# Three stages of a one-core, eight-layer kernel: gating cut into pieces, a last phase split by 128-row blocks, and a sixteenth of the softmax exponentials moved from ScalarE to VectorE

## What is computed

```python
# first attention: 16 heads, a window of 64 earlier rows, learned "bond" and "damage" logits
strain = disp_win - disp[:, :, :, None, :]
bond_act = gelu(strain @ W_strain + rel_emb @ W_pos)
damage = sigmoid((gelu(strain @ W_dmg + b_dmg) @ W_dmg_out)[..., 0] + b_dmg_out[0])
logits = (bond_act @ W_bond)[..., 0] - 10.0 * damage      # masked before row 0
out = einsum('bntd,bntde->bnte', softmax(logits), val_win) @ W_cproj

# gated layer: 8 experts, the one of the largest gate logit modulo 8
probs = softmax(x @ Wg + bg); idx = argmax(probs); p = probs[idx]
h = relu(einsum('bsd,edf->besf', x, We) + be)
out = h[expert idx % 8] * p

# last attention: 16 heads of 8, 2048 keys by 2048 queries
attn = softmax(q @ k.T * d ** -0.5) * (s / sqrt(s - 1.0))
out = (attn @ v) * s ** -0.5 ; out @ w_o.T * hid ** -0.5
```

## Time and profile before

| | us |
|---|---|
| median of 3 runs (2976.29 to 2985.98) | 2984.93 |
| the profiled execution's own time | 2982.17 |
| its span, first to last instruction | 2980.4 |

### The profile page before, as it was taken

How to read it: one execution, slowest core, us unless ns; L and a number is a source line. 1 busy time by engine, 2 the same in 40 slices (tenths; PEclk the granted TensorE clock), 3 DMA queues, 4 the chain that set the end, 5 groups by cost and what they waited for, 6 DMA issues and landing times. The chain is left out here.

```text
span 2980.4 us, 33149 instructions
## 1 busy us (share of the span) xinstructions
PE 2389.2 (80%) x12605; PEld 833.9 (28%) x12605; DVE 1860.6 (62%) x2713; ACT 2010.5 (67%) x2036; POOL 1070.7 (36%) x408
## 2 busy tenths in 40 slices
PE   3677777757666666766999889998769789999995
PEld 1122222334222222333222241222434422222223
DVE  5788898857999999864888528896350401112114
ACT  4999999813633333234899758997431379999991
POOL 5999999711099999531001300013000000000000
PEclk8899999978888888787999998999889889999997
DMA  2012111110144444102202100101010120210001
GB/s 75 1 43 62 67 43 43 43 53 8 28 176 168 163 162 152 68 4 78 41 12 37 35 7 1 18 6 45 8 40 0 35 65 18 41 27 18 15 6 28
DMA packets 64985, 144.64 MB, mean 49 GB/s; under 512 B 13091, under 2 KB 27791, under 8 KB 64112
## 3 DMA queue, kind: packets, MB, share of 16 engines
q1 hardware_dynamic: 64816, 142.40, 16.5%
HBM read 117.92 MB, written 24.25 MB: 48 GB/s over the span
## 5 line engine op out<-in xcount | busy, mean ns | idle before, releaser
L674 POOL TENSOR_TENSOR l0a_diff_pool<-l0a_A,l0a_a_of_t 128x2048 f32<-128x2048 f32 x128 | 531.7, 4191 | 34.3 <-ACT l0a_a_of_t L689 33.0
L1933 ACT ACTIVATE l2x_pT<-ps 128x1024 f32<-128x1024 f32 x512 | 495.7, 1021 | 14.5 <-PE ps L1892 12.6
L1933 ACT ACTIVATE l3he_pT<-ps 128x1024 f32<-128x1024 f32 x512 | 496.0, 1021 | 6.5 <-PE ps L1892 4.6
L1262 PE MATMUL ps<-l1s_hc,all_ident 128*128 128x512 f32 x512 | 288.7, 718 | 153.2 <-POOL l1s_hc L1233 97.6
L657 DVE SCALAR_TENSOR_TENSOR l0a_diff_dve<-l0a_A,l0a_pos,ps 128x512 f32<-128x512 f32 x512 | 344.8, 741 | 29.7 <-PE ps L532 29.7
L1224 POOL TENSOR_TENSOR l1s_dBx<-l1a_dtx,l1a_Bs 128x1024 f32<-128x1024 f32 x128 | 297.7, 2357 | 111.9 <-POOLq L958 111.9
L1248 ACT ACTIVATE ps<-l1a_dt,l1a_A 128x1024 f32<-128x1024 f32 x128 | 143.0, 1118 | 268.0 <-DVE l1s_hc L1307 215.7
L1892 PE MATMUL ps<-l2m_Qs,l2m_Ks 75*128 75x512 bf16 x1024 | 273.9, 392 | 9.8 <-PEq L2215 9.8
L1892 PE MATMUL ps<-l3h_Qs,l3h_Ks 75*128 75x512 bf16 x1024 | 269.3, 386 | 12.8 <-DVE ps L1981 12.8
L1906 PE MATMUL ps<-l2x_pT,l2m_Va 128*9 128x512 f32 x2048 | 272.5, 605 | 1.2 <-ACT l2x_pT L1933 1.2
L1906 PE MATMUL ps<-l3he_pT,l3h_Va 128*9 128x512 f32 x2048 | 269.2, 598 | 0.6 <-ACT l3he_pT L1933 0.6
(11 more groups left out here) (462 smaller groups left out, 3347.8 us busy)
## 6 DMA issues: line engine op xcount, KB each, us to landing
l1a_Bs<-l1a_bc SPq DMA_DIRECT2D x64, 512.0 KB, 3.6
l1s_Cs<-l1a_bc SPq DMA_DIRECT2D x64, 512.0 KB, 4.8
l0a_band_rows<-l0a_band SPq DMA_DIRECT2D x32, 512.0 KB, 5.2
l0a_band<-l0a_exps SPq DMA_DIRECT2D x16, 512.0 KB, 5.1
l2m_Ks<-l2m_parts SPq DMA_DIRECT2D x36, 128.0 KB
l2m_Qs<-l2m_parts SPq DMA_DIRECT2D x72, 64.0 KB
l3h_Qs<-l3h_parts SPq DMA_DIRECT2D x72, 64.0 KB
l0a_band<-l0a_zero SPq DMA_DIRECT2D x8, 512.0 KB, 4.8
```

Of the source, the lines that this page charges most:

```text
L674: pool.tensor_tensor(out, window(s), atb[:, p % 2, :].unsqueeze(1).broadcast_to([P, 4, CH]), ALU.subtract).then_inc(diff_pool, 1)
L1262: mm = pe.matmul(g.ps[:, (4 + 2 * h + q) * CH:(5 + 2 * h + q) * CH], g.ident[:, :], hc[:, m % NHC, q * CH:(q + 1) * CH], start=(n == 0), s ...
L1933: act.activation(pT[:, turn % NPT, :], g.ps[:, slot * QC:(slot + 1) * QC], ACT.Exp).then_inc(expd, 1)
```

## The change

It does three things.

1. **Last attention.** In each segment key block 7 leaves the sequence. ACT makes the exponentials of 15 blocks; the four turns of block 7 go to DVE, one after each of the blocks at places 0, 3, 6 and 9. Their scores are put behind two other turns' scores in PE's list; DVE reads them out of PSUM (`taken`), and makes the exponential as a power of two and a polynomial in ten instructions over 128x1024. The values of block 7 are multiplied right behind those at places 13 (first half of the columns) and 14 (second half). `finish` of the segment before now stands behind the four exponentials on DVE.
2. **First attention.** Only the last phase's end is rewritten, by blocks: each block's exponential as soon as its maxima are subtracted (four of 128x512), its own two DRAM writes, its own load; SP's order is write 0, write 1, load 0, write 2, load 1, write 3, load 2, load 3. Normalising, transposing, projecting and adding go by pairs of blocks. On DVE the copies of the phase before for units 0 to 3 come before the last logits, those for 4 to 7 after the maxima.
3. **Gated layer.** `gate` is cut into four pieces; one piece for the next quarter follows each block's `choose`. ACT's exps(q) moves behind mask(4q + 1), probability(q) behind choose of the second block, and `y` gets 4 places.

```diff
@@ bond_attention, PE, after the last slot: instead of tail(w, off) for two more phases
+                for i in range(4):
+                    values(LAST - 1, i)
+                for b in range(LB):
+                    logits_transpose(LAST, b)
+                for i in range(4, BU):
+                    band_transpose(LAST - 1, i)
+                for i in range(4, BU):
+                    values(LAST - 1, i)
+                for b in range(4):
+                    for i in (2 * b, 2 * b + 1):
+                        band_transpose(LAST, i)
+                    if b == 2:
+                        late_o_transpose(0)
+                    if b == 3:
+                        late_project(0)
+                    for i in (2 * b, 2 * b + 1):
+                        values(LAST, i)
+                late_o_transpose(1)
+                late_project(1)
@@ VectorE
+                for i in range(4):
+                    band_copy(LAST - 1, i)
+                logits(NT // TPG - 1)
+                for b in range(LB):
+                    subtract_max(LAST, b)
+                for i in range(4, BU):
+                    band_copy(LAST - 1, i)
+                normalise(LAST - 1)
...
+                late_add(0)
+                late_normalise(1)
+                late_o_copy(1)
+                late_add(1)
@@ ScalarE
-                exps(NPH - 1)
+                for b in range(LB):
+                    act.wait_ge(emptied, use("l", LAST, b) + 1)
+                    act.activation(E[:, b, :, :], E[:, b, :, :], ACT.Exp).then_inc(late_exp, 1)
@@ SyncE
+                def load(b):
+                    sp.wait_ge(late_written[b], 32)
+                    sp.wait_ge(filled, use("b", LAST - 1, 2 * b + 1) + 1)
+                    sp.dma_start(bn[:, b, :, :].rearrange("p u h -> p (u h)"), band[LAST % 2, b]).then_inc(loaded[b], 16)
+                write(0)
+                write(1)
+                load(0)
+                write(2)
+                load(1)
+                write(3)
+                load(2)
+                load(3)
@@ gated_experts
-        y = r.sb("y", [P, 2, C])
+        y = r.sb("y", [P, 4, C])
...
-                exps(0)
                 for q in range(NCH):
                     onehot_copy(q)
                     mask(4 * q + 1)
+                    exps(q)
                     bias_copy(q)
-                    if q + 1 < NCH:
-                        exps(q + 1)
                     mask(4 * q + 3)
...
-                gate(0)
+                gate_parts = (gate_max, gate_equal, gate_first, gate_hot)
+                for part_of_gate in gate_parts:
+                    part_of_gate(0)
                 for q in range(NCH):
-                    if q + 1 < NCH:
-                        gate(q + 1)
-                    for b in range(4 * q, 4 * q + 4):
-                        choose(b)
-                        if b == 4 * q:
+                    for b in range(4):
+                        choose(4 * q + b)
+                        if b == 1:
                             probability(q)
+                        if q + 1 < NCH:
+                            gate_parts[b](q + 1)
@@ head_attention, PE
+                for m in range(NBLK):
+                    seg, kt = divmod(m, ABLK)
+                    for c in range(2):
+                        if m + 1 < NBLK:
+                            block_scores(m + 1, 2 * c)
+                            block_scores(m + 1, 2 * c + 1)
+                        if c and kt in TAKEN:
+                            d = TAKEN.index(kt)
+                            scores(vector_turn(seg, d), seg, ABLK, d)
...
+                        values(seg, kt, c, lambda j: pT[:, (4 * m + j) % NPT, :])
+                        if kt == VECTOR_AT and c == 1:
+                            pe.wait_ge(vexpd, 4 * (seg + 1))
+                            values(seg, ABLK, 0, lambda j: dT[:, j, :])
+                        if kt == VECTOR_AT + 1 and c == 0:
+                            values(seg, ABLK, 1, lambda j: dT[:, j, :])
@@ VectorE
+                def exponential(seg, d):
...
+                    dve.tensor_scalar(y2[:, :], g.ps[:, slot(turn)], LOG2E, -126.0, ALU.mult, ALU.max).then_inc(taken, 1)
+                    dve.wait_ge(taken, 4 * seg + d + 1)
+                    step(dve.tensor_scalar(n2[:, :], y2[:, :], ROUND, None, ALU.add))
+                    step(dve.scalar_tensor_tensor(y2[:, :], n2[:, :], ROUND, y2[:, :], ALU.subtract, ALU.subtract))
+                    step(dve.tensor_scalar(n2[:, :].bitcast(I32), n2[:, :], ROUND - 127.0, 8388608.0, ALU.subtract, ALU.mult))
...
+                    step(dve.tensor_scalar(r, y2[:, :], EXP2[5], EXP2[4], ALU.mult, ALU.add))
+                    step(dve.tensor_tensor(r, r, y2[:, :], ALU.mult))
+                    for k in (3, 2, 1):
+                        step(dve.scalar_tensor_tensor(r, r, EXP2[k], y2[:, :], ALU.add, ALU.mult))
+                    dve.scalar_tensor_tensor(r, r, EXP2[0], n2[:, :], ALU.add, ALU.mult).then_inc(vexpd, 1)
...
                 for seg in range(NSEG):
+                    for d in range(4):
+                        exponential(seg, d)
                     if seg:
                         finish(seg - 1)
```

More of the change, by code:

```diff
@@ L711, in _ @@
                 sp.wait_ge(band_zeroed, 16 * 8)
-                for p in range(NPH):
+                for p in range(LAST):
                     sp.wait_ge(expd, p + 1)
@@ L1946, in head_attention, with slot @@
         sps, expd, accr = r3.sem("scores_in_psum"), r3.sem("exp_done"), [r3.sem("acc_read0"), r3.sem("acc_read1")]
+        taken, vexpd = r3.sem("scores_taken"), r3.sem("vector_exp_done")
         pvd = [r3.sem("pv_done0"), r3.sem("pv_done1")]
         steps, azero, kept, back = r3.sem("steps"), r3.sem("acc_zeroed"), r3.sem("sums_stored"), [r3.sem("sums_loaded0"), r3.sem("sums_loaded1")]
+        NBLK = NSEG * ABLK
+        reader = {}
+        for m in range(NBLK):
+            for j in range(4):
+                reader[act_turn(m, j)] = (expd, 4 * m + j + 1)
+        for seg in range(NSEG):
+            for d in range(4):
+                reader[vector_turn(seg, d)] = (taken, 4 * seg + d + 1)
+        assert sorted(reader) == list(range(4 * TB * NSEG))
+        LATE_KEYS = act_turn(TB // 2 - 1, 0)
+        def slot(turn):
+            return slice(turn % NST * QC, (turn % NST + 1) * QC)
         with nc.Block() as block:
@@ L1954, in _, with scores @@
                 pe.wait_ge(azero, 1)
-                head_segments(pe, g, hd, pT, sps, expd, accr, pvd, 0, NSEG)
+                def scores(turn, seg, kt, j):
+                    hg, qc = divmod(seg, NQ)
+                    if turn >= NST:
+                        sem, n = reader[turn - NST]
+                        pe.wait_ge(sem, n)
+                    if kt == 0 and j == 0:
+                        pe.wait_ge(hd.q_in[qc], hd.QIN * (hg + 1))
+                        if qc == 0:
+                            pe.wait_ge(hd.k_in[hg % 2], hd.KIN * (hg // 2 + 1))
+                    if turn == LATE_KEYS:
+                        pe.wait_ge(hd.k_late, hd.KIN)
+                    bank = slot(turn).start
+                    for c in range(QC // CH):
+                        mm = pe.matmul(g.ps[:, bank + c * CH:bank + (c + 1) * CH], hd.Ks[:, hg % 2, j, keys_of(kt) * P:(keys_of(kt) + 1) * P],
+                                       hd.Qs[:, qc, j, c * CH:(c + 1) * CH], start=True, stop=True)
+                    mm.then_inc(sps, 1)
@@ new lines, in block_scores, with values @@
+                def block_scores(m, j):
+                    seg, kt = divmod(m, ABLK)
+                    scores(act_turn(m, j), seg, kt, j)
+                def values(seg, kt, c, pick):
+                    hg = seg // NQ
+                    for j in range(4):
+                        mm = pe.matmul(g.ps[32 * j:32 * j + HS + 1, ACC + c * CH:ACC + (c + 1) * CH],
+                                       hd.Va[:, keys_of(kt), hg * 4 + j, :], pick(j)[:, c * CH:(c + 1) * CH],
+                                       start=(kt == 0), stop=(kt == ABLK - 1))
+                    mm.then_inc(pvd[c], 1)
@@ new lines, in _ @@
+                for j in range(4):
+                    block_scores(0, j)
+                for m in range(NBLK):
+                    seg, kt = divmod(m, ABLK)
+                    for c in range(2):
[5 more added lines that the diff above has]
+                            scores(vector_turn(seg, d), seg, ABLK, d)
+                        if c == 0:
+                            pe.wait_ge(expd, 4 * m + 4)
+                        if kt == 0 and seg:
+                            pe.wait_ge(accr[c], seg)
+                        values(seg, kt, c, lambda j: pT[:, (4 * m + j) % NPT, :])
[4 more added lines that the diff above has]
+                            values(seg, ABLK, 1, lambda j: dT[:, j, :])
@@ L1975, in _ @@
             def _(act):
-                head_exps(act, g, pT, sps, expd, pvd, 0, NSEG)
+                for m in range(NBLK):
```

(8 more changed lines are left out.)

104 lines of the change are left out of this document (90 added, 14 removed).

## The result

The changed kernel takes 2967.2 us (median of 5 runs, 2957.3 to 2969.5); the kernel before took 2986.0 in the same comparison (5 runs, 2976.3 to 2989.3). The two medians are 18.8 us apart; the ratio estimated from the runs is 0.9923, 95% interval 0.9901 to 0.9944: faster by 17 to 30 us. The forecast was 2953, range 2933 to 2969. The sign is right and the time lies inside the range, but 1.8 us from its far end: 31 us were expected, and 19 to 23 came, by the medians and by the ratio.

What follows compares the result with a forecast made beforehand. PE was taken to bound the last attention; the first attention's end was a lone chain, and engines took turns in the gated layer. From 2982.17 (profiled) or 2984.93 (median), -4 - 14 - 13 = -31 gave 2953, range 2933 to 2969.

Steps and rivals of the forecast that it cites:

- PE bounds the last attention: Last attention: PE sets the pace at 3.89 us a block; four changes between matmul kinds go per segment, -4 us.
- the rival in which ACT is the bound: Last attention: ACT sets the pace, so 32 exponentials fewer save 31 us, whole time 2927; chance 0.12.
- VectorE's exponential: Last attention: DVE's ten instructions take 10.9 us a turn, 12.6 at most, turns come every 12.1, so it hides.
- The rival of VectorE as the bound: Last attention: a DVE segment is 4T + 9.2 us (T one exponential), exceeding PE's 61.8 above T = 13.1; chance 0.06.
- First attention's end: Last phase by blocks: end near 613 against 626.99, -14 us, range -8 to -17 from slower or faster round trips.
- Its two units cost (621.42 - 611.17) / 8 = 1.28 each: First attention's end: two units of the last block, landing at about 606, cost 1.28 us each, giving 608.6.
- Gated layer: First one-hot to last add, 66.3 us before, gets shorter by 14.5, taken as -13; range -6 to -15.
- The sum: Whole kernel: -4 - 14 - 13 = -31 us, forecast 2953.
- The small-gains rival: First attention's loads wait in SP's list, gated layer's clock falls: -8, -6 and -4 are -18, about 2966; chance 0.12.
- A write of 128 KB: First attention's end: a block's small DRAM write is written about 3.7 us after issue, placed between 3.2 and 6.4.

Runs made afterwards that it cites:

- `e_short_exps`: Kernel before, with every exponential of the last attention on 768 of its 1024 columns and the weights filled with 1 once: 2997.2 us, one run.
- `e_first`: Kernel before with only the first attention's end changed: 2977.1 us, ratio 0.9964.
- `e_best`: Changed kernel with short matmuls of unread results on PE in the first attention's end, gated layer's first exponentials ahead of ACT's first mask: 2952.1 us, ratio 0.9879.
- `e_half_values`: Kernel before, with every value matmul of the last attention on 256 of its 512 columns: 3196.6 us, one run.
- `e_alternate`: Kernel before, with PE's last-attention list alternating one turn's scores with two heads' values, instead of two turns' with four heads': 3253.8 us, one run.

## Why the prediction was right or wrong

- **PE bounds the last attention; ACT's full record is overlap.** Right, and shown by `e_short_exps`. The gain is the four changes between kinds per segment: -4 forecast, -3.9 between the two profiles, -3.2 between the means. The 31 us of the rival in which ACT is the bound didn't come. The cost of a change, 0.11 us, was found again in two other orders of work.
- **VectorE's exponential.** 10.9 us forecast, 11.0 measured, each of the kinds as priced (1.22, 0.69). Turns every 12.1. It hides.
- **The rival of VectorE as the bound.** Its form was right, its threshold was too high: the 2.03 us at a segment's start were missing (12.7 instead of 13.1).
- **First attention's end.** The step that failed is "Its two units cost (621.42 - 611.17) / 8 = 1.28 each": a block is 2.56 us by it, and 3.7 to 4.1 came. The stretch that it was taken from runs at the full clock for its last 6 us only, from 615 on; all of the new stretch ran at 0.50. The maxima, exponentials and first load came where I had put them, within 1.2 us (591.29 for 590.2, 596.32 for 596.0), the last load about two later (604.3 for 602.2). I had let the end hang on that load. In the run PE was the bound instead: its queue of blocks let it begin the last one at 612.17, not at 606.
- **The clock behind the removed wait.** I had counted the wait that goes as pure gain, and not looked at the clock behind it: in the kernel before it rose at 615, while PE ran 24 transposes in a row. In all six profiles of that order it rose 3 to 6 us after the first of these transposes. In the five of the new order it fell between 597 and 600, and rose before the stage's end in one (`e_first`) only. What raises it is not settled beyond that. That its level is the reason is shown by `e_best`: with the clock held, this part is worth 13 us against my 14. As changed it is 7 to 8. That this lies at the near edge of my -8 to -17 is luck: I had made that bound out of slower round trips, and the first of them was faster.
- **Gated layer.** -13 forecast, -13.2 in the pair of profiles, but -9 over all. The new stage was priced well (54.75 us against 51.8 by the working, 53.3 with my allowance; the quarter 12.96 against 12.4, in part since VectorE's small instructions lengthen beside GpSimd's: 0.30 us for one that takes 0.17 where GpSimd is idle). What was off is the old one: 66.3 us from a profile in which the stage was 4 us longer than in four others.
- **The sum.** By the differences of the means the forecast was 6 us off in the first attention, 4 in the gated layer, 1 in the last attention and 4 in the dual attention, all to the same side: together the 14 us between 2953 and 2967.
- **The small-gains rival** (2966, 0.12), which had the clock staying low as its mechanism, comes nearest in time. It named the gated layer for it, where PE kept its full clock in the profile; it came true in the first attention, for which the rival had its right number (-8) by loads waiting in SP's list, and PE waited 0.72 us for them.
- **A write of 128 KB.** Forecast from bounds 3.7 us for the round trip; from the first issue at 593.39 to the load at 596.32 it is 2.9. The row of after:

```profile
l0a_band<-l0a_exps SPq DMA_DIRECT2D x8, 128.0 KB, 2.9
```

The Trainium skill, DMA: Bandwidth & Descriptors, Anatomy of one DMA, would give about 2.3 us for it (an estimate from its formula, which is a fit of DMAs issued in another way, from GpSimd): nearer than my bounds, still 0.6 short.

## What to carry to other kernels

Before you count a removed wait of PE as gain, look at the granted clock behind it, and price the work that follows at both levels: a stretch that ran at full clock in the old order may not do so in the new one. When two engines both look full, tell the bound from the distance of starts, and from the pace of the other engine where its input was made ahead. And take a stage's length from several profiles before you divide a small gain among stages: the same code differed by 4 us in 86.

## What the runs showed of the hardware that I had not expected

- PE with open matmuls all the time can stay at half clock: 12.00 of 12.00 us at 0.50 in the changed kernel, 16.00 of 16.00 in `e_first`, and the last attention of `e_half_values`. Halving the columns of half of the matmuls made that stage 213 us slower.
- Value matmuls of two heads into two 32-row places take as long (0.86 us) as those of four into four.
- A change between the score matmuls and the value matmuls costs 0.10 to 0.11 us on PE: 0.54 - 0.43 in `e_alternate` at 1.00, and (2.79 - 2.59) / 2 in `e_half_values` at 0.50, there an estimate with matmuls taken as twice as long.
